# Expert loops: up products transposed, their weights copied by ScalarE, the transposes of the hidden activations dropped

## What is computed

```python
xn = rms_norm(x, norm_scale)
scores_topk, idx = jax.lax.top_k(xn @ w_router.T, 2)       # 8 experts
weights = jax.nn.softmax(scores_topk, axis=-1)
up = moe_linear(xf, ids, w_up)             # each token's expert: 128 -> 512
u, gate = jnp.split(up, 2, axis=-1)
h = u * jax.nn.silu(gate)                  # 256 hidden channels
down = moe_linear(h, ids, w_down)          # 256 -> 128
out = jnp.sum(down * weights[..., None], axis=-2)
```

## Time and profile before

| | us |
|---|---|
| median of 3 runs | 1284.92 |
| lowest, highest run | 1284.26, 1287.82 |
| span of the profiled execution, first to last instruction | 1267.4 |
| TensorE matmul busy (share of span) | 1039.7 (82%) |
| ScalarE busy | 805.9 (64%) |
| VectorE busy | 657.0 (52%) |
| GpSimd busy | 373.5 (29%) |
| granted TensorE clock, mean | 0.923 |

### The profile page before, as it was taken

How to read it: one execution, slowest core, us unless ns; L and a number is a source line. 1 busy time by engine, 2 the same in 40 slices (tenths; PEclk the granted TensorE clock), 3 DMA queues, 4 the chain that set the end, 5 groups by cost and what they waited for, 6 DMA issues and landing times. The chain is left out here.

```text
span 1267.4 us, 23481 instructions
## 1 busy us (share of the span) xinstructions
PE 1039.7 (82%) x8814; PEld 493.5 (39%) x8846; DVE 657.0 (52%) x2128; ACT 805.9 (64%) x1164; POOL 373.5 (29%) x376
## 2 busy tenths in 40 slices
PE   4369988998999999989978988778887885997930
PEld 3242222322222232222156655444544554664620
DVE  5753656376365435323156436668767773633522
ACT  4338887988899999989924745555444442474520
POOL 2100210211110111434010644234431273364435
PEclk9689998999999999999998999789888997998975
DMA  5270370027037500200011333100000011234422
GB/s 147 48 115 1 59 105 2 2 51 108 7 64 135 145 1 19 114 24 26 22 38 51 115 98 92 41 18 16 16 16 1 8 39 53 82 106 114 131 64 66
DMA packets 84829, 74.76 MB, mean 59 GB/s; under 512 B 11440, under 2 KB 78896, under 8 KB 83824
## 3 DMA queue, kind: packets, MB, share of 16 engines
q1 hardware_dynamic: 74924, 55.46, 20.0%
q0 software_dynamic: 8192, 16.79, 4.6%
q10 hardware_dynamic: 1604, 0.99, 0.3%
HBM read 39.26 MB, written 33.95 MB: 58 GB/s over the span
## 5 line engine op out<-in xcount | busy, mean ns | idle before, releaser
L1301 ACT ACTIVATE attn_probs<-ps 128x1024 f32<-128x1024 f32 x512 | 484.6, 1066 | 58.5 <-PE ps L1012 57.1
L1029 PE MATMUL ps<-attn_probs,attn_v 128*18 128x512 f32 x2048 | 272.2, 604 | 9.2 <-DVE room L1260 8.6
L1672 POOL DMA_INDIRECT slots<-moe_xr,moe_slot x128 | 124.3, 971 | 169.0 <-ACT attn_probs L1301 64.9
L1012 PE MATMUL ps<-stack 50*128 50x512 bf16 x1024 | 165.0, 386 | 8.4 <-ACT attn_probs L1301 2.0
L1683 POOL DMA_INDIRECT moe_back<-results,moe_slot x128 | 123.4, 964 | 120.4 <-PE ps L1728 50.0
L1738 PE MATMUL ps<-stack,lin_scores 128*128 x312 | 154.5, 618 | 0.1
L1012 PEld LDWEIGHTS ps<-stack 50*128 50x128 bf16 x1024 | 34.4, 94 | 244.3 <-ACT attn_probs L1301 226.6
L1844 ACT ACTIVATE lin_scores<-ps 128x256 f32<-128x256 f32 x156 | 58.3, 381 | 98.9 <-PE ps L1738 98.9
L1817 DVE TENSOR_TENSOR lin_scores<-ps,lin_scores 128x256 f32<-128x256 f32 x156 | 59.0, 418 | 109.2 <-ACT lin_scores L1844 109.1
L1764 PE MATMUL ps<-stack,lin_scores 128*128 x624 | 85.2, 280 | 4.8 <-ACT lin_heads_out L1857 4.8
L1764 PEld LDWEIGHTS ps<-stack,lin_scores 128*128 128x128 f32 x624 | 77.7, 195 | 6.5 <-issue 6.5
(11 more groups left out here) (235 smaller groups left out, 1520.7 us busy)
## 6 DMA issues: line engine op xcount, KB each, us to landing
moe_gathered<-slots SPq DMA_DIRECT2D x76, 128.0 KB, 2.4
results<-lin_heads_out SPq DMA_DIRECT2D x76, 128.0 KB
stack<-qk_parts SPq DMA_DIRECT2D x36, 256.0 KB, 9.1
qk_parts<-moe_xr SPq DMA_DIRECT2D x32, 128.0 KB, 3.0
qk_parts<-moe_xr SPq DMA_DIRECT2D x16, 192.0 KB, 2.8
stack<-in_expert_w SPq DMA_DIRECT2D x1, 3072.0 KB, 10.4
slots<-zeros SPq DMA_DIRECT2D x1, 3008.0 KB, 12.5
slots<-zeros SPq DMA_DIRECT2D x1, 2496.0 KB, 20.8
```

What stands on the lines that cost most here:

```text
L1012: instruction = T.matmul(k.ps[:, SCORE_BANKS[i % 3][s], :], d.stack[b % 2][rows, 1, pair, kt * P:(kt + 1) * P], d.stack[b % 2][rows, 0, pa ...
L1029: instruction = T.matmul(k.ps[32 * j:32 * j + STRIP, PV_BANK, :], d.v[:, b % 2, kt, first:first + STRIP], d.probs[:, n % A_PROBS, j * BANK ...
L1301: A.activation(d.probs[:, n % A_PROBS, 2 * e * BANK:2 * (e + 1) * BANK], k.ps[:, banks[0]:banks[1] + 1, :].rearrange("p a n -> p (a n)"), ...
L1672: G.indirect_dma_start(out=k.dram["slots"][half][0:SLOT_TILES[r] * P], out_offset=bass.IndirectOffsetOnAxis(ap=d.slot[:, FIRST[r] + at, c: ...
```

## The change

The up product is turned round. For each tile and each of the four 128-column chunks of its expert's up weights, one matmul takes the weights as the stationary operand and the turned tokens as the moving one, so the result has the experts' inner channels along the partitions. It is in the layout that the down product needs, so `turn_hidden`, its bank and its copy are dropped. The stationary weights are read at a fixed place: ScalarE copies each tile's 512 weight columns from `expert_w`, at an offset that it loads into a register itself, to `d.up`, two buffers of a unit each. It does so for unit 0 ahead of the loop and for unit u+1 in iteration u, after silu(u-1). TensorE waits for the copy of unit u (`e_weights`) ahead of the last transpose of turn(u). The down product moves from iteration u+3 to u+2 (`DOWN_LAG`) and alternates between banks 6 and 7; the stores move with it.

```diff
@@ plan_loop
-        if 0 <= u - 2 < UNITS[r]:
-            k.banks.fill(("eht", r, u - 2), 6)
-        if 0 <= u - 3 < UNITS[r]:
-            k.banks.fill(("edown", r, u - 3), 7)
+        if 0 <= u - DOWN_LAG < UNITS[r]:
+            k.banks.fill(("edown", r, u - DOWN_LAG), DOWN_BANKS[(u - DOWN_LAG) % 2])
@@ pe_loop, turn
         for i in range(unit_width(r, u)):
+            if i == unit_width(r, u) - 1:
+                T.wait_ge(k.e_weights, UNITS_BEFORE[r] + u + 1)
             instruction = T.transpose(k.ps[:, bank, i * P:(i + 1) * P], k.moe.gathered[:, u % NG, i, :], k.ident[:, :])
@@ pe_loop, up
-            T.matmul(k.ps[:, bank, :], d.gt[:, u % NB, i, :], w[:, bass.ds(offset[u, i], 2 * HIDDEN)], start=True,
-                     stop=True).then_inc(k.full[bank], 1)
+            for c in range(UP_CHUNKS):
+                instruction = T.matmul(k.ps[:, bank, c * P:(c + 1) * P], d.up[u % NB][:, i, c * P:(c + 1) * P],
+                                       d.gt[:, u % NB, i, :], start=True, stop=True)
+            instruction.then_inc(k.full[bank], 1)
@@ pe_loop, turn_hidden removed; down
-        h_bank, h_n = k.use["eht", r, u]
-        if u == 0:
-            T.wait_ge(k.free[h_bank], h_n + 1)
...
         for i in range(unit_width(r, u)):
+            u_bank, u_n = k.use["eup", r, u, i]
+            T.wait_ge(k.free[u_bank], u_n + 1)
             for c in range(2):
-                instruction = T.matmul(k.ps[:, bank, i * DIM:(i + 1) * DIM], d.ht[:, u % NB, i, c * P:(c + 1) * P],
+                instruction = T.matmul(k.ps[:, bank, i * DIM:(i + 1) * DIM], d.h[:, u % NB, i, c * P:(c + 1) * P],
@@ pe_loop, act_loop, order of an iteration
-        if 0 <= u - 2 < UNITS[r]:
-            turn_hidden(u - 2)
-        if 0 <= u - 3 < UNITS[r]:
-            down(u - 3)
+        if 0 <= u - DOWN_LAG < UNITS[r]:
+            down(u - DOWN_LAG)
@@ act_loop
+    w = k.expert_w.rearrange("p e c -> p (e c)")
+    A.wait_ge(k.e_offsets, r + 1)
+    A.wait_ge(k.expert_in, 16)
+
+    def weights(u):
+        for i in range(unit_width(r, u)):
+            j = u * UNIT + i
+            offset = A.value_load(k.moe.offsets[0:1, r % 2, j:j + 1], min_val=0, max_val=(EXPERTS - 1) * EXPERT_COLS)
+            instruction = A.activation(d.up[u % NB][:, i, :], w[:, bass.ds(offset, 2 * HIDDEN)], ACT_FN.Copy)
+        instruction.then_inc(k.e_weights, 1)
...
+    weights(0)
     for u in range(UNITS[r] + 3):
...
             silu(u - 1)
+        if u + 1 < UNITS[r]:
+            weights(u + 1)
@@ sp_loop
-        if 0 <= u - 3 < UNITS[r]:
-            store(u - 3)
+        if 0 <= u - DOWN_LAG < UNITS[r]:
+            store(u - DOWN_LAG)
@@ loop_buffers
-    d.silu, d.h, d.ht = (room[:, i * NB:(i + 1) * NB, :].rearrange("p b (i c) -> p b i c", i=UNIT) for i in range(3))
+    d.silu, d.h = (room[:, i * NB:(i + 1) * NB, :].rearrange("p b (i c) -> p b i c", i=UNIT) for i in range(2))
+    d.up = [room[:, 2 * NB:2 * NB + UNIT, :], sums[:, :, :]]
```

More of the change, by code:

```diff
@@ L55 @@
 EXPERT_COLS = 2 * HIDDEN + HIDDEN // P * DIM
+UP_CHUNKS = 2 * HIDDEN // P
 assert not any(units % NG for units in UNITS) and LOOP_TILES in (SIZES[2], 16)
@@ L76 @@
 SCORE_BANKS, PV_BANK, AUX = ((0, 1), (2, 3), (4, 5)), 6, 7
-SIDE_BANK = 1
+SIDE_BANK, DOWN_BANKS, DOWN_LAG = 1, (6, 7), 2
 A_LAG, A_PROBS, VALUES_AT = 2, 3, 7
@@ L1844, in silu @@
             A.activation(d.silu[:, u % NB, i, :], k.ps[:, bank, HIDDEN:2 * HIDDEN], ACT_FN.Silu).then_inc(k.e_silu, 1)
[L1846 to L1851, removed]
     def down(u):
@@ L2401, in experts_buffers, with loop_buffers @@
     return d
-def loop_buffers(nc, ctx, room, heads_out):
+def loop_buffers(nc, ctx, room, heads_out, sums):
     d = Stage(nc, ctx, "loop")
@@ L2475, in macaron_kernel @@
             k.lin = linear_buffers(nc, late, k)
-            k.loop = loop_buffers(nc, late, k.lin.scores, k.lin.heads_out)
+            k.loop = loop_buffers(nc, late, k.lin.scores, k.lin.heads_out, k.lin.sums)
             k.back = late.enter_context(nc.sbuf_tensor("moe_back", [P, RING, TOPK, DIM], F32))
@@ L2506, in macaron_kernel @@
         k.expert_in = signal("expert_in")
-        k.e_xr, k.e_both, k.e_gap, k.e_gap_act, k.e_slots, k.e_offsets, k.e_silu, k.e_kept, k.e_merged = (
-            signal("e_" + n) for n in ("xr", "both", "gap", "gap_act", "slots", "offsets", "silu", "kept", "merged"))
+        k.e_xr, k.e_both, k.e_gap, k.e_gap_act, k.e_slots, k.e_offsets, k.e_silu, k.e_kept, k.e_merged, k.e_weights = (
+            signal("e_" + n) for n in ("xr", "both", "gap", "gap_act", "slots", "offsets", "silu", "kept", "merged", "weights"))
         k.e_gather, k.e_store, k.e_back = signals("e_gather", NG), signals("e_store", NG), signals("e_back", RING)
```

## The result

The changed kernel takes 1337.8 us (median; 1329.9 to 1339.7) against 1284.6 for the kernel before: a ratio of 1.040 (95% interval 1.036 to 1.043), **53 us slower**. The forecast was 1311, slower, with a range of 1296 to 1345. The direction and the mechanism came out; the size, 53 us, is twice the forecast's 26.

A forecast was written before the change was run, and what follows sets the result against it. TensorE was taken to bound the plain unit at 3.27 us, and a ring through ScalarE's copies to bind afterwards at 3.78. Terms of about +26 us added to the 1284.9 median gave 1311, range 1296 to 1345.

The forecast's parts named there:

- the plain unit: Two 128-token tiles in an expert loop without side work or late loads; 50 such intervals at +0.51 us: +25.5.
- the clock case: Rival, 8%: TensorE's idle of 0.9 us per unit lowers its clock in a third of plain units; about 1343 us.
- the serial one: Rival, 17%: ScalarE's register loads wait until its previous instruction ends; unit 4.27 to 4.67 us, total 1337 to 1360.
- TensorE's own time: TensorE's work alone per plain unit after the change: 2.89 us, 0.38 less than before.
- The ring: Per unit: up product, Silu, register load, two copies, TensorE's restart at turn(u)'s second transpose, next up product; 3.78 us against 3.27.
- the register load on ScalarE: Load of the weight offset before each copy: 0.35 us plus 0.05 address arithmetic, 0.15 not hidden by the Silu.
- The starts of loops: First units of each loop now wait for ScalarE's copies too: +7 us in all, +2.1 of it in loop 0.
- The ends of loops: Shorter tail after a loop's last up product: -2.6 us in loops 0 and 3, -0.5 in loop 2, together -5.7.
- Side units: Ten units with other TensorE work or a VectorE wait cover the added wait and save 0.44 us of transposes: -4.4.
- late loads: Seven units already held to 3.5 to 3.8 us by late loads: +1 us.
- The keep pieces: Sixteen pieces of 1.64 us on ScalarE, with its work running a little late, 0.15 us each: +2.4.
- The ring doesn't bind: Rival, 8%: ScalarE's stretch stays under 1.00 us, TensorE never waits, a plain unit takes 2.89 us; total 1256.

The follow-up runs named there:

- `wait_at_up`: Changed kernel with TensorE's wait for the copied weights moved from the second transpose of turn(u) to ahead of up(u): 1276.6 us, 0.990 of the kernel before.
- `copies_once`: Changed kernel with ScalarE's weight copies left out except for the first two units of each loop, wait still at the turn: 1278.5 us, 0.990 of the kernel before.
- the first profile of before: Unchanged kernel before, first profiled execution: span 1267.4 us; profiled a second time, span 1286.8 us.
- `changed_again`: Changed kernel unaltered, run once more on one chip beside two variants: 1337.4 us, 1.037 of the kernel before.
- `after`: First profile of the changed kernel, nothing else altered: median 1337.8 us, 1.040 of the kernel before.
- `copies_in_eighths`: Changed kernel with each tile's 512-column weight copy on ScalarE cut into eight of 64 columns, wait still at the turn: 1495.9 us, 1.163 of the kernel before.

## Why the prediction was right in kind and short in size

**What bounds the kernel: right.** TensorE bounded the plain unit, and almost nothing but the loops moved.

**The range: met by the part lent from the rivals.** The measured 1337.8 lies outside the forecast's own 1298 to 1325. It is inside 1296 to 1345 only because that range took in the clock case and half of the serial one, and neither is what happened in the plain units.

**TensorE's own time: right.** 2.89 us per unit forecast, 2.90 in `wait_at_up` and `copies_once`; 16 passes forecast at 1.78 us, 1.79 in the trace, with their weight loads hidden.

**The ring: right in mechanism, 0.31 us short.** Term by term, forecast and trace of the changed kernel: end of up to Silu 0.20 and 0.20; second Silu to the first copy 0.40 and 0.62; two copies 1.15 and 1.26; copy's end to TensorE 0.14 and 0.05; transpose to the first up pass 0.11 and 0.17; up product 1.78 and 1.79. Sum 3.78 and 4.09. The step that failed is the register load on ScalarE with its address arithmetic: 0.35 + 0.05 us in the forecast, which left 0.15 beyond the Silu and nothing beyond the copy. The trace shows both parts when asked for the line of `value_load`. ScalarE's sequencer in the unit above (duration in ns min/median/max, first and last start in us):

```profile
L1835 ACTq TENSOR_LOAD <-moe_offsets x1: 273/273/273, 1152.2 to 1152.2; - x1
L1835 ACTq FUSED_REGOPS  x1: 152/152/152, 1152.5 to 1152.5; - x1
L1835 ACTq SEQ_ASSERT  x1: 18/18/18, 1152.7 to 1152.7; - x1
```

The load begins with the Silu at 1152.20 and takes 0.27 us, less than I took. The arithmetic and check behind it, and another 0.04 us of arithmetic on the copy's own line, bring the copy to 1152.82: 0.35 us where I had put 0.05. The load of the second copy begins behind the first copy's start and takes as long in all, 0.63 us, longer than the copies' pitch of 0.52. So the two cost the unit 0.46 us, and two runs show it: without loads, and with the loads earlier, the unit is 3.63. The first delays the first copy by 0.34 us, the second takes away the overlap of the copies, 0.12 us. Even the upper end of 3.96 was too low. Times the forecast's 50 plain units that is +41 us where the sum had +25.5. Fewer were plain: 41 intervals took 3.2 to 3.4 us in the first profile of before (starts of loops aside; 38 in the second), and they grew by 35.8 (33.1) us. I treated an idle time of TensorE as the bound for the load. The trace of the kernel before had TensorE's loads themselves:

```profile
L1774 PEldq TENSOR_LOAD <-moe_offsets x156: 294/301/605, 633.3 to 1206.3; - x156
L1774 PEldq FUSED_REGOPS  x156: 146/151/151, 633.7 to 1206.7; - x156
```

From the start of such a load to the end of its check is 0.59 us in the median. Put in place of 0.40 it would have given 0.34 beyond the Silu and 0.07 beyond the copy, a ring of 4.04 (an estimate from these rows), near the 4.09 measured.

**The starts of loops: half of what they cost.** Forecast +7, measured 14: the first two intervals grow from 5.5 to 10.5 us in loop 0, from 6.3 to 10.5 in loop 1, from 6.4 to 11.2 in loop 3. In the earlier trace rows I added a ring at full clock. But loops 1 and 3 begin after a wait for transfers, with the clock at its lower level, and an up product in the ring takes nearly twice as long. Start of loop 3 in the changed kernel, timeline of TensorE:

```profile
1200.93 3.62 PE L1740 MATMUL ps<-lin_scores 128*128 128x128 f32 x16
...
1206.54 0.47 PE L1729 MATMUL ps<-c_ident,moe_gathered 128*128 128x128 f32 x1 [1.77 <-ACT lin_scores L1836]
1206.80 3.15 PE L1740 MATMUL ps<-lin_scores,lin_sums 128*128 128x128 f32 x16
...
1212.11 1.06 PE L1740 MATMUL ps<-lin_scores 128*128 128x128 f32 x8
```

The up products at 1200.93 and 1206.80 last 3.62 and 3.15 us, and the wait of 1.77 us stands between them. The kernel before has one slow up product there and no wait behind it, and the second is fast already:

```profile
1148.53 3.52 PE L1738 MATMUL ps<-stack,lin_scores 128*128 x4
1151.88 0.38 PE L1728 MATMUL ps<-c_ident,moe_gathered 128*128 128x128 f32 x2
1152.10 1.88 PE L1738 MATMUL ps<-stack,lin_scores 128*128 x4
```

Loop 0 shows the part of the clock. In `changed_again` it began with the clock at 1.00, and its first two intervals are the bare ring, 4.11 and 4.10 us, where the first profile of the changed kernel had slow up products and 5.06 and 5.43:

```profile
642.31 1.96 PE L1740 MATMUL ps<-lin_scores 128*128 128x128 f32 x16
```

That start costs 2.7 us more than before, the other 4.9; the forecast had 2.1.

**The ends of loops: -5.7 forecast, -2.4 measured against the first profile of before, -4.2 against the second.** The end of loop 3 gave 2.5 us, as forecast (2.6). The end of loop 0 gave nothing; its timeline in the changed kernel:

```profile
745.78 1.06 PE L1740 MATMUL ps<-lin_scores,lin_sums 128*128 128x128 f32 x8
...
749.66 0.28 ACT L1849 ACTIVATE lin_heads_out<-ps 128x128 f32<-128x128 f32 x1 [1.17 <-PE ps L1754]
...
750.41 5.05 SPq L1899 DMA_DIRECT2D moe_gathered<-slots  x5
```

The last copy ends at 749.94, 4.16 us after the last up product began (5.65 before, 3.06 forecast), because the last Silu began late, for a reason that the profile doesn't give. And the next loop's first tile, loaded at 750.41, was there only at 754.38, 4.0 us later; in the first profile of before it took 2.3. Which of the transfers around it was in its way wasn't tested.

**Side units as forecast, late loads not.** Interval by interval against the first profile of before (the second in brackets), the nine units of 4.5 us and more got 4.6 (3.0) us shorter, where the sum had -4.4. But the ten (eleven) intervals of 3.4 to 3.9 us, for which the sum had +1, grew by 5.6 (6.1): the ring of 4.09 is above them too. The keep pieces can't be told apart; they are in these figures.

**The base: a wrong reading without a consequence.** I took the 17.5 us between span and median for what lies around the span. It is 1.8 us; the rest was the short linear stage of that one execution, which kept the higher clock for longer. Since the sum was added to the median, the forecast didn't suffer.

**The rivals.** Serial loads (17%): the times that it gave, 1337 to 1360, hold the measured one, and the loads were indeed dearer than forecast. But its mechanism is refuted: the load begins with the Silu and not behind it, the second one with the first copy, and the unit is 4.09, under its 4.27. So that these times fit is no merit of that rival. The clock (8%): not in the plain units of the changed kernel, at work at its starts of loops, and in every loop with a longer ring. The ring doesn't bind (8%): refuted as a forecast, and `wait_at_up` shows that it would have given a gain, of 11 to 16 us, not the 29 that I put on it: irregular units take the rest.

## What to carry to other kernels

A wait costs by what stands behind it on its engine's queue: put it directly ahead of the first instruction that reads the data, and when work moves to another engine, walk once round the ring of that wait before adding up busy times. Here the same added work was worth -1% or +4% by the place of one wait. Where an engine loads a register for an instruction behind a wait, place the load ahead of that wait: here it took 0.46 us off each plain unit. The length of a load is read from the trace by its line in the source, address arithmetic included. And profile the kernel before twice, and compare the granted clock, before reading a stage's length from it.

## What the runs showed of the hardware that was not expected

- A register load on ScalarE took 0.28 us in the median, but with the address arithmetic and the range check behind it the instruction that uses it began 0.62 us after the load. Between a Silu and its copy it began with the Silu and put the copy at 0.62 us after the Silu's start, 0.28 without the load; a second one removed the overlap of two copies of 0.63 us (1.26 us for two, 1.14 without). Issued ahead of the wait for the up product the loads cost nothing (3.63 us a unit, as without loads).
- TensorE kept the clock at 1.00 over 40 us with an idle of 0.97 us in each unit of 4.09 (`after`, 1130 to 1170), and had 0.80 in the mean with 2.4 us of idle in a unit of 5.5 to 7.4 (`copies_in_eighths`, 1200 to 1280).
- The linear stage of one and the same kernel took 269.2 us in one profile and 286.3 in another, at a mean granted clock of 0.88 and 0.82.
